# Layer statistics per group instead of per batch of four, and Q and Wo projections interleaved with attention mixing

## The chip, the cores and the metric

One Trainium2 chip, all eight cores; every core runs the same program on its own half of one of four sequences. The metric is the device time in microseconds of the slowest core.

## The reference, cut to what matters

```python
xn = layernorm(x)                                  # (4, 4096, 1024)
def attn(x):
    K = elu(x @ Wk + bk) + 1;  Q = elu(x @ Wq + bq) + 1;  V = x @ Wv + bv    # 16 heads of 64
    KV = einsum('nshd,nshm->nhmd', K, V);  Ksum = K.sum(axis=1)
    Z = 1 / (einsum('nlhd,nhd->nlh', Q, Ksum) + 1e-6)
    out = einsum('nlhd,nhmd,nlh->nlhm', Q, KV, Z) @ Wo + bo
    x = layernorm(x + out) * g1 + beta1
    return layernorm(x + relu(x @ W1 + b1) @ W2 + b2) * g2 + beta2
def experts(x):                                    # 8 experts of width 4096, two per token by a hash of x[:, :2]
    return sum(w[e] * (relu(x @ W1[e] + b1[e]) @ W2[e] + b2[e]) for e in range(8))
out = x + attn(xn) + experts(xn)
```

## The kernel before, in words

A core has 2048 own tokens (`TOWN`, 16 groups of 128, `NGOWN`) and needs K and V of all 4096 tokens of its sequence (32 groups, `NG`). The program is written by hand: the builder emits each engine's instructions in the order of the code, and each engine runs its own list strictly in that order. `em` adds an instruction, `inc` lets it raise a semaphore, `wait` puts a wait in the list, `chain` and `vbar` make an engine wait for its own last instruction. In the code T is TensorE, V VectorE, S ScalarE, G GpSimd (weight loads) and Y the sync engine SP (row loads). `barrier` stands between the stages.

The stages, in order: phase A (statistics, normalization, transposition, K and V, and the sum KV), its tail (routing of the tokens), the experts (`emit_moe`), B1 (`emit_b1`: Q, the attention mixing, Wo), a layernorm, the feed-forward (`emit_b2`), a second layernorm, and the output (`emit_b4`). The change is in phase A and B1 alone.

**Phase A** (`emit_phase_a`) goes by groups, and by batches of four groups for the statistics. Four slots of `xtm_a` hold the rows. For one group g:

- `stats_sums(g)` loads the rows (SP; the slot is free when the transposes of g-4 are done), takes their sum on VectorE (L406) and scales it (L408); ScalarE squares the centred rows (L413) and subtracts the mean (L415); VectorE sums the squares (L418), and for own groups copies the mean (L423).
- `stats_finish` does the rest of the variance for four groups at once: one VectorE scaling (L432), Ln and Exp on ScalarE (L435, L437), four small VectorE operations (L440 to L446), and then on ScalarE for each of the four groups the scaling of the rows (L454) and three one-column copies for own groups (L457 to L461).
- `emit_trans(g)` transposes the eight 128x128 blocks on TensorE (L505) in two waves through one PSUM bank, each copied out by ScalarE (L516).
- `emit_proj(g)` is the K matmuls (L527), a bias row (L531), the V matmuls (L539) and a bias row (L543).
- `elu_all(g)` is the maximum on VectorE (L474), the exp on ScalarE (L482), the min-add (L487) and the copy of V (L493) on VectorE.
- `emit_kv(g)` is sixteen small matmuls (L558, L561), which VectorE adds to the running sums (L573 to L575).

In the loop each group g of a batch is emitted as transposes, projections, `stats_sums` of group g+4, elu, KV, and `stats_finish` of the next batch follows the fourth group. Before the loop stand four `stats_sums` and a `stats_finish`. All group-local buffers of elu and KV have two slots.

**B1** works on two halves s of 1024 own tokens. First the Q projection of both halves, eight output blocks n each (L832, 16 matmuls, with the elu in pieces of 512 columns: L845, L850, L854). Then for each half: the mixing, twice (`sub`, 512 columns each): eight denominator matmuls (L876), an addition and a reciprocal on VectorE (L882, L887), and for each of eight head pairs p a matmul that spreads the reciprocal (L894), a ScalarE copy (L900), the mixing matmul (L904) and a VectorE product (L911); then a reload and transposition of the normalized rows (L933, L941, L948); and the Wo projection, eight blocks (L962, with L972 on VectorE). The copy `xnfm` of the normalized rows lies over `xnbf`, the operand of the Q projection, so it can't be written before the last Q matmul.

Of the kernel before, what the change touches and what calls it, by code (L numbers as in the profile page):

```python
# [6 lines left out]
F32 = mybir.dt.float32  # L7
BF16 = mybir.dt.bfloat16
# [60 lines left out]
class KB:  # L69
    def __init__(self, debug=(), ngl=NG, alim=6, moe_e=NEXP, moe_y=True, gser=False, moe_wb=True, emod=NEXP, hblk=10000):  # L70
# [19 lines left out]
        self.s_lx = [mk("lx0"), mk("lx1"), mk("lx2"), mk("lx3")]  # L90
# [69 lines left out]
    def _decl_sbuf(self):  # L160
# [8 lines left out]
        self.sq2 = sb("sq2", [128, 2 * D], F32, 49664, 65536)  # L169
# [9 lines left out]
        self.xtm_a = sb("xtm_a", [128, 4 * D], F32, TR, 196608)  # L179
        self.ktm = sb("ktm", [128, 2 * D], BF16, TR + 16384, 196608)  # L180
        self.vtm = sb("vtm", [128, 2 * D], BF16, TR + 20480, 196608)
        self.elu_a = sb("elu_a", [128, 2 * D], F32, TR + 24576, 196608)
# [50 lines left out]
        self.scol = sb("scol", [128, 8], F32, SZ + 768)  # L233
# [142 lines left out]
    def emit_phase_a(self):  # L376
        ps = self.ps
        NGL = self.ngl
        assert NGL % 4 == 0
        evT = {}; evKV = {}; evKVmm = {}; evA = {}; evXN = {}  # L380
        evK_s = {}; evK_v = {}; evV_v = {}; evDMA = {}; evSQ = {}
        evKmm = {}; evVmm = {}
        evXNw = [0]

        def lhs(c, g):
            if g < NGOWN:
# [3 lines left out]
        def stats_sums(g):  # L390
            own = g < NGOWN
            bpar = (g // 4) % 2
            j = g % 4
            col = bpar * 4 + j
            sl = g % 4
            xt = self.xtm_a[:, sl * D:(sl + 1) * D]
            if g >= 4:
                self.wait("Y", self.s_mm, evT[g - 4])
            evDMA[g] = self.dma("Y", xt, self.xs[g * 128:(g + 1) * 128, :], self.s_lx[g % 4])
            mc = self.scol[:, col:col + 1]  # L400
            ac = self.tpack[:, col:col + 1]
            sq = self.sq2[:, (g % 2) * D:(g % 2 + 1) * D]
            self.wait("V", self.s_lx[g % 4], evDMA[g])
            if g >= 2:
                self.wait("V", self.s_ve, evSQ.get(g - 2, 0))
            self.em("V", lambda v: v.reduce_sum(mc, xt, axis=AXX))  # L406
            self.vbar()
            self.em("V", lambda v: v.tensor_scalar_mul(mc, mc, -INV_D))  # L408
            v_negm = self.inc("V", self.s_ve, 1)
            self.wait("S", self.s_ve, v_negm)  # L410
            if g >= 2:
                self.wait("S", self.s_ve, evSQ.get(g - 2, 0))
            self.em("S", lambda s: s.activation(sq, xt, AF.Square, bias=mc))  # L413
# [896 lines left out]
```

How the kernel before makes its waits and increments, by code:

```python
    def wait(self, e, sem, val):  # L243
        if val > 0:
            self.L[e].append(lambda x, s=sem.h, v=val: x.wait_ge(s, v))
            self.meta[e].append(("wait", sem.name, val))
# [4 lines left out]
        def fn(x, prev=prev, s=sem.h, n=n):  # L251
            prev(x).then_inc(s, n)
```

## Time and profile before

| | us |
|---|---|
| profiled execution, slowest core | 6002.73 |
| its span, first to last instruction (core 4) | 6001.2 |
| timed runs | 6006.98 and 6708.36 |
| their median | 6357.67 |
| phase A: first to last group's transposes | 69.8 to 714.9 |
| experts, first to last matmul | some 800 to 4550 |
| B1 | 4555 to 4940 |

The page gives TensorE 4866.0 us of matmuls (81% of the span), VectorE 1709.8 (28%), ScalarE 1090.0 (18%) and GpSimd 345.8 (6%). The shares are means over stages with different limits, so the prediction reads phase A, the experts and B1 apart. "Granted clock" is the share of TensorE's full 2.4 GHz that the chip let it have.

### The profile page before, as it was taken

The numbers are of one execution on the slowest core, as the hardware profiler recorded it, in microseconds if no ns is written. First come the engines' busy times: TensorE is split into PE (matmuls) and PEld (weight loads), VectorE is DVE, ScalarE is ACT, GpSimd is POOL, SyncE is SP. The second block draws the span as 40 slices with busy tenths as digits, with TensorE's granted clock in tenths as the row PEclk, the third lists the DMA queues.
The fourth block names the chain that finished last, engine by engine and source line by source line (L and its number), as shares of the span: only waits on it lengthen the run. The fifth ranks groups of instructions, "written<-read, shape, count | busy, mean of one in ns | idle before, by whom it ended". The sixth has DMA issues, their size and how long they took to land.

```text
span 6001.2 us, 55303 instructions; the slowest of 8 cores (5960.0 to 6001.2 us)
## 1 busy us (share of the span) xinstructions
PE 4866.0 (81%) x21246; PEld 2145.8 (36%) x21665; DVE 1709.8 (28%) x3231; ACT 1090.0 (18%) x2013; POOL 345.8 (6%) x661
## 2 busy tenths in 40 slices
PE   3565559999999999999999999999996442677752
PEld 1222224444444444444444444444432110233311
DVE  2333312222222222222222222222223225111153
ACT  2333221111111111111111111111111123111120
POOL 1000000000000000000000000000000000000000
PEclk8777789999999999999989999999998665999965
DMA  2000012222222222222222222222212110111103
GB/s 58 25 25 25 11 26 38 38 36 38 39 36 38 39 36 37 39 36 38 39 32 34 39 36 37 39 36 37 38 30 36 42 39 0 28 26 27 26 7 112
DMA packets 105681, 209.46 MB, mean 35 GB/s; under 512 B 12960, under 2 KB 13232, under 8 KB 105424
## 3 DMA queue, kind: packets, MB, share of 16 engines
q0 software_dynamic: 91056, 163.84, 18.0%
q1 hardware_dynamic: 14368, 42.06, 2.1%
q8 instruction: 177, 2.90, 0.2%
q14 instruction: 80, 0.66, 0.0%
HBM read 361.06 MB, written 8.39 MB: 62 GB/s over the span
## 4 chain that ended last, share of the span: by engine, by line
PE 73%; DVE 11%; ACT 7%; DMA 5%; issue 4%; DVEq 0%; POOL 0%; ACTq 0%; SPq 0%; POOLq 0%
PE ps L735 30%; PE ps L773 30%; PE ps L1099 4%; PE ps L1120 4%; DMA xtm_a<-xs 2%; DMA xt_b<-xs 1%; ACT h_b L1109 1%; DMA xtm_b<-xs 1%; PE ps L779 1%; DVE x_sb L1137 1%; PE ps L505 1%; DVE ln_t L1059 1%; DVE ktm L487 1%; DVE vtm L493 1%; DVE elu_a L474 1%
## 5 line engine op out<-in xcount | busy, mean ns | idle before, releaser
L735 PE MATMUL ps<-xnbf,w1s 128*128 128x512 bf16 x8027 | 1829.1, 383 | 63.9 <-DVE wb L720 32.7
L735 PEld LDWEIGHTS ps<-xnbf,w1s 128*128 128x128 bf16 x8192 | 803.2, 99 | 1057.9 <-issue 150.1
L773 PE MATMUL ps<-h_hi,w2s 128*128 128x512 bf16 x4008 | 929.9, 388 | 27.8 <-DVE acc L797 22.9
L773 PE MATMUL ps<-h_lo,w2s 128*128 128x512 bf16 x4015 | 901.5, 379 | 4.3
L797 DVE TENSOR_TENSOR acc<-acc,ps 128x512 f32<-128x512 f32 x992 | 615.1, 682 | 851.3 <-PE ps L773 535.4
L773 PEld LDWEIGHTS ps<-h_hi,w2s 128*128 128x128 bf16 x4096 | 407.5, 100 | 531.5 <-issue 90.8
L745 ACT ACTIVATE h_lo<-ps,eb_sb 128x512 bf16<-128x512 f32 x512 | 310.2, 688 | 1565.9 <-PE ps L735 1565.9
L745 ACT ACTIVATE h_hi<-ps,eb_sb 128x512 bf16<-128x512 f32 x512 | 310.2, 688 | 1467.3 <-PE ps L735 1467.3
L773 PEld LDWEIGHTS ps<-h_lo,w2s 128*128 128x128 bf16 x4096 | 401.0, 98 | 484.6 <-issue 4.9
L753 DVE TENSOR_TENSOR h_lo<-h_lo,wb 128x512 bf16<-128x512 bf16 x512 | 183.3, 420 | 961.0 <-ACT h_lo L745 961.0
L753 DVE TENSOR_TENSOR h_hi<-h_hi,wb 128x512 bf16<-128x512 bf16 x512 | 183.3, 420 | 900.9 <-ACT h_hi L745 900.9
L1099 PE MATMUL ps<-c_bf,w1s 128*128 128x512 bf16 x1003 | 238.8, 395 | 100.9 <-ACT h_b L1109 76.0
L1120 PE MATMUL ps<-h_b,w2s 128*128 128x512 bf16 x1004 | 234.7, 390 | 92.7 <-DVE x_sb L1137 59.1
L293 POOL DMA_DIRECT2D w2s<-ew_pk x256 | 135.7, 530 | 1751.4 <-PE ps L773 1188.4
L293 POOL DMA_DIRECT2D w1s<-ew_pk x256 | 135.9, 531 | 1705.3 <-PE ps L735 1705.3
L505 PE MATMUL ps<-ident,xtm_a 128*128 128x128 f32 x256 | 64.5, 402 | 168.9 <-ACT xn L461 86.7
L1099 PEld LDWEIGHTS ps<-c_bf,w1s 128*128 128x128 bf16 x1024 | 101.5, 101 | 238.9 <-issue 133.4
L1120 PEld LDWEIGHTS ps<-h_b,w2s 128*128 128x128 bf16 x1024 | 100.2, 100 | 227.2 <-issue 119.6
L1137 DVE TENSOR_TENSOR x_sb<-x_sb,ps 128x512 f32<-128x512 f32 x96 | 59.5, 682 | 421.8 <-PE ps L1120 421.8
L1109 ACT ACTIVATE h_b<-ps,b_sb 128x512 bf16<-128x512 f32 x128 | 77.5, 688 | 491.8 <-PE ps L1099 491.8
L941 PE MATMUL ps<-ident,xt_b 128*128 128x128 f32 x128 | 34.8, 428 | 117.6 <-DVE xt_b L933 117.6
L558 PE MATMUL ps<-vtm,ktm 128*128 128x128 bf16 x256 | 31.0, 239 | 104.3 <-DVE vtm L493 104.3
(169 smaller groups left out, 2250.6 us busy)
## 6 DMA issues: line engine op xcount, KB each, us to landing
w1s<-ew_pk POOLq DMA_DIRECT2D x256, 256.0 KB, 3.8
w2s<-ew_pk POOLq DMA_DIRECT2D x256, 256.0 KB, 3.8
xtm_a<-xs SPq DMA_DIRECT2D x32, 512.0 KB, 3.3
xt_b<-xs SPq DMA_DIRECT2D x32, 256.0 KB, 2.6
w1s<-w_pk POOLq DMA_DIRECT2D x32, 256.0 KB, 3.9
w2s<-w_pk POOLq DMA_DIRECT2D x32, 256.0 KB, 3.9
xtm_b<-xs SPq DMA_DIRECT2D x16, 512.0 KB, 4.0
out<-otm_b SPq DMA_DIRECT2D x16, 512.0 KB, 2.9
```

Source lines behind the costliest of these rows:

```text
L293: self.em(e, lambda x, o=out, i=in_: x.dma_start(out=o, in_=i))
L474: self.em("V", lambda v, hh=hh: v.tensor_scalar(rt[:, hh * 512:(hh + 1) * 512], ps[hh][:], 0.0, None, op0=OP.max))
L505: self.em("T", lambda t, c=c, j=j: t.transpose(ps[4][:, j * 128:(j + 1) * 128], xt[:, c * 128:(c + 1) * 128], self.ident[:]))
L735: self.em("T", lambda t, k=k, tt=tt, slot=slot: t.matmul(ps[tt][:], self.w1t(slot, k), self.xnbf[:, k * TOWN + tt * 512:k * TOWN + (tt + 1 ...
L745: self.em("S", lambda s, tt=tt, i=i, hreg=hreg, e=e, n=n: s.activation(hreg[:, i * TOWN + tt * 512:i * TOWN + (tt + 1) * 512], ps[tt][:], ...
L753: self.em("V", lambda v, tt=tt, i=i, hreg=hreg, e=e: v.tensor_mul(hreg[:, i * TOWN + tt * 512:i * TOWN + (tt + 1) * 512], hreg[:, i * TOWN ...
L773: self.em("T", lambda t, j=j, tt=tt, slot=slot, hreg=hreg, lp=last_plain: t.matmul(ps[4 + tt][:], self.w2t(slot, j), hreg[:, j * TOWN + tt ...
L797: self.em("V", lambda v, dst=dst, tt=tt: v.tensor_add(dst, dst, ps[4 + tt][:]))
L1099: self.em("T", lambda t, k=k, tt=tt, slot=slot: t.matmul(ps[tt][:], self.w1t(slot, k), self.c_bf[:, k * TOWN + tt * 512:k * TOWN + (tt + 1 ...
L1109: self.em("S", lambda s, tt=tt, i=i, n=n: s.activation(self.h_b2[:, i * TOWN + tt * 512:i * TOWN + (tt + 1) * 512], ps[tt][:], AF.Relu, bi ...
L1120: self.em("T", lambda t, j=j, tt=tt, slot=slot: t.matmul(ps[4 + tt][:], self.w2t(slot, j), self.h_b2[:, j * TOWN + tt * 512:j * TOWN + (tt ...
L1137: self.em("V", lambda v, x=xsl, tt=tt: v.tensor_add(x, x, ps[4 + tt][:]))
```

## The change

**Phase A.** The batches go. `emit_stats(g)` computes the whole statistic of one group; `xtm_a` has two slots instead of four, and the squares lie in the slot of `elu_a` instead of a buffer of their own. VectorE keeps the two sums and two scalings. Ln, Exp and the five operations that finish the reciprocal deviation are now all on ScalarE, on one column, each waiting for the one before; the row scaling follows. The mean and the deviation of own groups are written in place, so two of the copies go. The statistic of group g+1 is emitted before KV of group g and its transposes, with the elu of g folded into it: the maximum stands ahead of the second sum on VectorE, the exp ahead of Ln on ScalarE. TensorE's order in phase A is the same as before.

**B1.** The code is cut into functions, and the order is: Q of half 0; Q of half 1 with the first mixing of half 0 behind block 3 and the second behind block 7; row reload of half 0; Wo of half 0 with the first mixing of half 1 behind block 3 and the second behind block 7; row reload of half 1; Wo of half 1. No instruction is added or left out.

```diff
-        self.s_lx = [mk("lx0"), mk("lx1"), mk("lx2"), mk("lx3")]
+        self.s_lx = [mk("lx0"), mk("lx1")]
...
-        self.sq2 = sb("sq2", [128, 2 * D], F32, 49664, 65536)
...
-        self.xtm_a = sb("xtm_a", [128, 4 * D], F32, TR, 196608)
+        self.xtm_a = sb("xtm_a", [128, 2 * D], F32, TR, 196608)
...
+            if g >= 2:
+                self.wait("Y", self.s_mm, evT[g - 2])
+            evDMA[g] = self.dma("Y", xt, self.xs[g * 128:(g + 1) * 128, :], self.s_lx[par])
+            mc = self.mstat[:, g:g + 1] if own else self.scol[:, 0:1]
+            rc = self.rstat[:, g:g + 1] if own else self.scol[:, 1:2]
...
+            self.em("V", lambda v, xt=xt, mc=mc: v.reduce_sum(mc, xt, axis=AXX))
+            self.vbar()
+            self.em("V", lambda v, mc=mc: v.tensor_scalar_mul(mc, mc, -INV_D))
...
+            self.em("S", lambda s, xt=xt, sq=sq, mc=mc: s.activation(sq, xt, AF.Square, bias=mc))
+            self.chain("S", self.s_sc)
+            self.em("S", lambda s, xt=xt, mc=mc: s.add(xt, xt, mc))
+            s_sub = self.inc("S", self.s_sc, 1)
+            if mid_v is not None:
+                mid_v()
+            self.wait("V", self.s_sc, s_sub)
+            self.em("V", lambda v, sq=sq, ac=ac: v.reduce_sum(ac, sq, axis=AXX))
+            self.vbar()
+            self.em("V", lambda v, ac=ac: v.tensor_scalar(ac, ac, INV_D, EPS_LN, op0=OP.mult, op1=OP.add))
+            v_ac = self.inc("V", self.s_ve, 1)
+            if mid_s is not None:
+                mid_s()
+            r0 = self.scol[:, 3:4]
+            self.wait("S", self.s_ve, v_ac)
+            self.em("S", lambda s, ac=ac, r0=r0: s.activation(r0, ac, AF.Ln))
+            self.chain("S", self.s_sc)
+            self.em("S", lambda s, r0=r0: s.activation(r0, r0, AF.Exp, scale=-0.5))
+            self.chain("S", self.s_sc)
+            self.em("S", lambda s, rc=rc, r0=r0: s.mul(rc, r0, r0))
+            self.chain("S", self.s_sc)
+            self.em("S", lambda s, rc=rc, ac=ac: s.mul(rc, rc, ac))
+            self.chain("S", self.s_sc)
+            self.em("S", lambda s, rc=rc: s.mul(rc, rc, self.nwc_sb[:, 0:1]))
+            self.chain("S", self.s_sc)
+            self.em("S", lambda s, rc=rc: s.add(rc, rc, self.nwc_sb[:, 1:2]))
+            self.chain("S", self.s_sc)
+            self.em("S", lambda s, rc=rc, r0=r0: s.mul(rc, rc, r0))
+            self.chain("S", self.s_sc)
+            self.em("S", lambda s, xt=xt, rc=rc: s.mul(xt, xt, rc))
...
+                emit_stats(g, mid_v=lambda pg=pg, ek=ek: elu_vmax(pg, ek),
+                           mid_s=lambda pg=pg, ek=ek, ev=ev: (elu_sexp(pg, ek),
+                                                             elu_vtail(pg, ev)))
+                emit_kv(pg)
...
+            ek, ev = emit_T(g)
+            pend.append((g, ek, ev))
...
+        for n in range(KC):
+            qproj_n(0, n)
+        for n in range(KC):
+            qproj_n(1, n)
+            if n == 3:
+                mix_sub(0, 0)
+            if n == 7:
+                mix_sub(0, 1)
+        xnrec(0)
+        for n in range(KC):
+            wo_n(0, n)
+            if n == 3:
+                mix_sub(1, 0)
+            if n == 7:
+                mix_sub(1, 1)
+        xnrec(1)
+        for n in range(KC):
+            wo_n(1, n)
```

ScalarE in phase A, from the copies of group 3 on, before (`ktm` is K after the exp, `tpack` and `scol` hold statistics, `xn` the first two columns):

```order
L516 CAST xnbf<-ps 128x128 x8
L413 ACTIVATE sq_50<-xtm_a,scol 128x1024
L415 ACTIVATE xtm_a<-xtm_a,scol 128x1024
L482 ACTIVATE ktm<-ps 128x512 x2
L435 ACTIVATE tpack<-tpack 128x4
L437 ACTIVATE tpack<-tpack 128x4
L454 ACTIVATE xtm_a<-xtm_a,scol 128x1024
L457 COPY rstat<-scol 128x1
L459 COPY xn_107<-xtm_a 128x1
L461 COPY xn_107<-xtm_a 128x1
```

and the same engine now, in every step of an own group:

```order
L407 ACTIVATE elu_a<-xtm_a,mstat 128x1024
L409 ACTIVATE xtm_a<-xtm_a,mstat 128x1024
L517 ACTIVATE ktm<-ps 128x512 x2
L422 ACTIVATE scol<-scol 128x1
L424 ACTIVATE scol<-scol 128x1
L426 ACTIVATE rstat<-scol 128x1
L428 ACTIVATE rstat<-rstat,scol 128x1
L430 ACTIVATE rstat<-rstat,nwc_sb 128x1
L432 ACTIVATE rstat<-rstat,nwc_sb 128x1
L434 ACTIVATE rstat<-rstat,scol 128x1
L436 ACTIVATE xtm_a<-xtm_a,rstat 128x1024
L439 COPY xn_106<-xtm_a 128x1
```

Seven one-column activations stand between the exp and the row scaling of each group; before, two on four columns stood there once in four groups.

VectorE in phase A before, one step (`kvacc`, `ksacc` are the running sums):

```order
L406 TENSOR_REDUCE scol<-xtm_a 128x1
L408 TENSOR_SCALAR scol<-scol 128x1
L418 TENSOR_REDUCE tpack<-sq_50 128x1
L423 COPY mstat<-scol 128x1
L474 TENSOR_SCALAR elu_a<-ps 128x512 x2
L487 SCALAR_TENSOR_TENSOR ktm<-ktm,elu_a 128x512 x2
L493 CAST vtm<-ps 128x512 x2
L573 TENSOR_TENSOR kvacc<-kvacc,ps 128x512
```

and now:

```order
L400 TENSOR_REDUCE mstat<-xtm_a 128x1
L402 TENSOR_SCALAR mstat<-mstat 128x1
L505 TENSOR_SCALAR elu_a<-ps 128x512 x2
L414 TENSOR_REDUCE scol<-elu_a 128x1
L416 TENSOR_SCALAR scol<-scol 128x1
L528 SCALAR_TENSOR_TENSOR ktm<-ktm,elu_a 128x512 x2
L534 CAST vtm<-ps 128x512 x2
L563 TENSOR_TENSOR kvacc<-kvacc,ps 128x512
```

The elu maximum (L474, now L505) no longer has both sums ahead of it, but the second sum now stands between it and the min-add.

TensorE in B1 at the end of the first mixing of half 0, before:

```order
L894 MATMUL ps<-zbfb,e_sb 128x512
L904 MATMUL ps<-q_sb,m_sb 128x512
L876 MATMUL ps<-q_sb,ksbd 16x512 x8
L894 MATMUL ps<-zbfb,e_sb 128x512
L904 MATMUL ps<-q_sb,m_sb 128x512
```

and now:

```order
L888 MATMUL ps<-zbfb,e_sb 128x512
L898 MATMUL ps<-q_sb,m_sb 128x512
L834 MATMUL ps<-xnbf,w1s 128x512 x64
L869 MATMUL ps<-q_sb,ksbd 16x512 x8
L888 MATMUL ps<-zbfb,e_sb 128x512
L898 MATMUL ps<-q_sb,m_sb 128x512
```

Sixty-four matmuls, the Q projection of blocks 4 to 7 of half 1, stand between the two mixings that followed each other before.

## Rows read from the trace of the kernel before

**Rows 1.** Stage table: stretch, its us, then busy us (instructions) by engine, clock, DMA.

```profile
240.00:325.00 85.00, 50.97 (x236) 23.31 (x240) 32.15 (x57) 27.01 (x66) 0.00 (x0) 0.74 0.08 25
...
2900.00:3000.00 100.00, 99.53 (x456) 45.34 (x464) 28.82 (x60) 17.78 (x30) 7.42 (x14) 1.00 0.26 40
...
3100.00:3200.00 100.00, 99.27 (x371) 39.59 (x377) 22.04 (x44) 12.12 (x20) 5.83 (x11) 0.81 0.19 30
```

**Rows 2.** Timeline (start us, us, what): TensorE's transposes of groups 0, 29 and 31.

```profile
69.79 1.09 PE L505 MATMUL ps<-ident,xtm_a 128*128 128x128 f32 x4 [69.79 <-ACT xn L461]
...
681.24 0.64 PE L505 MATMUL ps<-ident,xtm_a 128*128 128x128 f32 x4
...
714.91 0.64 PE L505 MATMUL ps<-ident,xtm_a 128*128 128x128 f32 x4
```

**Rows 3.** Waits of phase A, and the row load's time to landing from the page.

```profile
DVE scol L406 <- DMA xtm_a<-xs: 192.6, 28, 14.9
...
xtm_a<-xs SPq DMA_DIRECT2D x32, 512.0 KB, 3.3
```

**Rows 4.** Timeline of the close of the third batch, up to the next transposes.

```profile
326.51 0.16 DVE L432 TENSOR_SCALAR tpack<-tpack 128x4 f32<-128x4 f32 x1
326.77 0.20 ACT L435 ACTIVATE tpack<-tpack 128x4 f32<-128x4 f32 x1 [5.88 <-DVE tpack L432]
...
328.44 1.15 ACT L454 ACTIVATE xtm_a<-xtm_a,scol 128x1024 f32<-128x1024 f32 x1 [1.17 <-DVE scol L446]
329.68 0.19 ACT L457 COPY rstat<-scol 128x1 f32<-128x1 f32 x1
329.96 0.19 ACT L459 COPY xn<-xtm_a 128x1 f32<-128x1 f32 x1
...
330.68 1.09 PE L505 MATMUL ps<-ident,xtm_a 128*128 128x128 f32 x4 [5.62 <-ACT xn L461]
```

**Rows 5.** Timeline of group 28, in the last batch: V matmuls and elu.

```profile
674.71 3.63 PE L539 MATMUL ps<-wv_sb,xnp 128*128 128x512 bf16 x16
674.96 1.29 DVE L474 TENSOR_SCALAR elu_a<-ps 128x512 f32<-128x512 f32 x2 [14.45 <-PE ps L531]
...
677.58 1.29 DVE L487 SCALAR_TENSOR_TENSOR ktm<-ktm,elu_a 128x512 bf16<-128x512 bf16 x2 [1.34 <-ACT ktm L482]
...
679.05 1.29 DVE L493 CAST vtm<-ps 128x512 bf16<-128x512 f32 x2 [0.17 <-DVE ktm L487]
```

**Rows 6.** Timeline of the start: table load and second sum of group 0.

```profile
42.98 1.28 ACT L413 ACT_TABLE_LOAD   x1 [42.98 <-DVE scol L408]
...
46.76 1.22 DVE L418 TENSOR_REDUCE tpack<-sq 128x1 f32<-128x1024 f32 x1 [3.86 <-ACT xtm_a L415]
48.08 0.15 DVE L423 COPY mstat<-scol 128x1 f32<-128x1 f32 x1
```

**Rows 7.** Groups of ScalarE: exp of 512 columns without and with an SBUF bias.

```profile
L482 ACT ACTIVATE ktm<-ps 128x512 bf16<-128x512 f32 x64 | 34.7, 594 | 119.6 <-DVE elu_a L474 119.6
...
L850 ACT ACTIVATE q_sb<-ps,bq_sb 128x512 bf16<-128x512 f32 x32 | 22.0, 687 | 179.0 <-DVE elu_r L845 177.2 <-PE ps L832 1.7
```

**Rows 8.** B1: timeline of the mixings of half 0 and 1; chain of waits (first Wo matmuls, reload).

```profile
4646.90 0.69 DVE L882 TENSOR_SCALAR ps<-ps 16x512 f32<-16x512 f32 x1 [3.83 <-PE ps L876]
...
4662.32 3.58 PE L876 MATMUL ps<-q_sb,ksbd 128*16 128x512 bf16 x8
...
4666.01 0.69 DVE L882 TENSOR_SCALAR ps<-ps 16x512 f32<-16x512 f32 x1 [2.64 <-PE ps L876]
...
4758.10 5.13 PE ps L962 x15
...
4790.67 1.89 PE L876 MATMUL ps<-q_sb,ksbd 128*16 128x512 bf16 x8
...
4828.83 2.71 DMA xt_b<-xs
```

**Rows 9.** Cores view: the die that did not hold the slowest core.

```profile
die 0 (median of its cores): 5973.9 us, clock 0.901
```

More of the change, by code:

```diff
@@ L411, in stats_sums @@
             if g >= 2:
-                self.wait("S", self.s_ve, evSQ.get(g - 2, 0))
-            self.em("S", lambda s: s.activation(sq, xt, AF.Square, bias=mc))
+                self.wait("S", self.s_mm, evKVmm.get(g - 2, 0))
+            self.em("S", lambda s, xt=xt, sq=sq, mc=mc: s.activation(sq, xt, AF.Square, bias=mc))
             self.chain("S", self.s_sc)
-            self.em("S", lambda s: s.add(xt, xt, mc))
+            self.em("S", lambda s, xt=xt, mc=mc: s.add(xt, xt, mc))
             s_sub = self.inc("S", self.s_sc, 1)
+            if mid_v is not None:
+                mid_v()
@@ L511, in emit_trans @@
                 self.wait("S", self.s_mm, mmv)
-                if (g >= NGOWN) and g >= 2:
+                if (not own) and g >= 2:
                     self.wait("S", self.s_mm, evKVmm.get(g - 2, 0))
@@ L546, in emit_proj, with elu_vmax @@
                     start=False, stop=True))
-            evVmm[g] = self.inc("T", self.s_mm, 1)
+            evVmm = self.inc("T", self.s_mm, 1)
+            return evKmm, evVmm
+        def elu_vmax(g, evKmm):
+            par = g % 2
+            rt = self.elu_a[:, par * D:(par + 1) * D]
+            self.wait("V", self.s_mm, evKmm)
+            if g >= 2:
+                self.wait("V", self.s_mm, evKVmm.get(g - 2, 0))
+            for hh in range(2):
+                self.em("V", lambda v, hh=hh, rt=rt: v.tensor_scalar(
+                    rt[:, hh * 512:(hh + 1) * 512], ps[hh][:], 0.0, None, op0=OP.max))
+            evK_v[g] = self.inc("V", self.s_ve, 1)
@@ new lines, in elu_sexp @@
+        def elu_sexp(g, evKmm):
+            par = g % 2
+            kslot = self.ktm[:, par * D:(par + 1) * D]
+            self.wait("S", self.s_mm, evKmm)
+            self.wait("S", self.s_ve, evK_v[g])
+            if g >= 2:
+                self.wait("S", self.s_mm, evKVmm.get(g - 2, 0))
+            for hh in range(2):
+                self.em("S", lambda s, hh=hh, kslot=kslot: s.activation(
+                    kslot[:, hh * 512:(hh + 1) * 512], ps[hh][:], AF.Exp))
+            evK_s[g] = self.inc("S", self.s_sc, 1)
@@ new lines, in elu_vtail @@
+        def elu_vtail(g, evVmm):
+            par = g % 2
+            kslot = self.ktm[:, par * D:(par + 1) * D]
+            vslot = self.vtm[:, par * D:(par + 1) * D]
+            rt = self.elu_a[:, par * D:(par + 1) * D]
+            self.wait("V", self.s_sc, evK_s[g])
+            for hh in range(2):
+                self.em("V", lambda v, hh=hh, kslot=kslot, rt=rt: v.scalar_tensor_tensor(
+                    kslot[:, hh * 512:(hh + 1) * 512], kslot[:, hh * 512:(hh + 1) * 512],
+                    1.0, rt[:, hh * 512:(hh + 1) * 512], op0=OP.min, op1=OP.add))
+            self.vbar()
+            self.wait("V", self.s_mm, evVmm)
+            for hh in range(2):
+                self.em("V", lambda v, hh=hh, vslot=vslot: v.tensor_copy(
+                    vslot[:, hh * 512:(hh + 1) * 512], ps[2 + hh][:]))
+            evV_v[g] = self.inc("V", self.s_ve, 1)
@@ L920, in emit_b1, with xnrec @@
+        def xnrec(s):
+            self.wait("T", self.s_sc, evZB[0])
+            self.wait("Y", self.s_ve, aoz_done[s])
             if s == 1:
```

395 lines of the change are left out of this document (155 added, 240 removed).

## The prediction

> **What bounds the kernel now.** I read the stage table first. In the mixture-of-experts stage TensorE is busy 99.5 of 100 us at a granted clock of 1.00, the upper of its two levels (1.2 and 2.4 GHz) [rows 1]. The change leaves that stage alone, so the edit can only win in phase A and in B1. In a batch of phase A (240 to 325 us) TensorE is busy 51 of 85 us, VectorE 32, ScalarE 27: no engine is full, the stage is a chain. Its length: the first transposes of group 0 start at 69.79, those of group 31 at 714.91 [rows 2]: 645.1 us over 31 steps, 20.8 each. The last batch (groups 28 to 31), beside which no statistics run, steps faster: transposes at 681.24 and, two groups later, at 714.91 [rows 2], 16.84 each. So some 4 us a step belong to how the statistics are placed. The waits show where: VectorE's first sum of a group waited for the row load 28 times, 192.6 us in all [rows 3] (the load waits for the transposes four groups back, so it lands in mid-projection, and the elu maximum is queued behind that whole statistic). And at each batch's end there is the close [rows 4]: from `stats_finish` at 326.51 to the next transposes at 330.68, 4.2 us in which TensorE has nothing, then four row scalings on ScalarE in front of the copies of the first group.
>
> **Phase A, a step of the changed kernel.** The per-step order on TensorE stays (transposes, K, V, KV), so I start from the last batch, which is a step without statistics. Measured from the elu maximum at 674.96: the min-add at +2.62, the copy of V at +4.09, the next transposes at +6.28 (681.24) [rows 5]. Now the statistics of group g+1 go around this. The row load has two slots and starts when the transposes of g-1 are done, most of a step (16.8 us) before its use, and takes 3.3 us to land [rows 3]: nothing waits. First sum, square and subtract run during transposes and K, hidden by TensorE. What lies on the path comes behind the maximum:
> - VectorE: the maxima take 1.29 for two, less an overlap: the second sum starts at +1.25. It takes 1.22 and a step of 1.32 to the next instruction (a sum at 46.76, the next at 48.08) [rows 6], so the one-column scaling starts at +2.57. The min-add, ready at +2.62, slips by under 0.1.
> - ScalarE: hand-off 0.26 (326.51 to 326.77); Ln takes 0.20 there and a copy 0.19, and copies follow each other by 0.28 (329.68, 329.96) [rows 4], so Ln and Exp are 0.29 each. Then five operations of one column with an operand in SBUF. No such row exists. Bounds: 0.28 each, as the copies, and 0.38: the form with an SBUF bias costs 0.093 more on 512 columns (687 against 594 ns) [rows 7]. Mul and add here read such an operand, so I take 0.38: 1.90 us. The row scaling takes 1.15, the signal to TensorE, an estimate, half a hand-off: 0.13. Sum: 2.57+0.26+0.58+1.90+1.15+0.13 = +6.59, against +6.28 for the KV path: 0.31 late. An own group (0 to 15) adds two copies at their spacing, 0.56: 0.87 late.
>
> So the new wait is the transposes on ScalarE's chain, 0.3 to 0.9 us a step; queued behind them is all of TensorE. Steps: 15 of 16.84+0.87 = 17.71 (groups 1 to 15) and 16 of 16.84+0.31 = 17.15: 265.7+274.4 = 540.1 us instead of 645.1, a gain of 105.0. With 0.28 an operation the chain is 0.5 shorter (own 17.21, other 16.84): 527.6, a gain of 117.5.
>
> The start: group 0 no longer waits for four statistics. Its second sum starts at 46.76 and the scaling at 48.08 [rows 6]; then 0.26+0.58+1.90+1.24 (the scaling's spacing, 328.44 to 329.68)+0.28+0.19+0.13 = 4.58 gives transposes at 52.7 instead of 69.79: gain 17.1. The step behind it is in the count above. Phase A's tail is unchanged.
>
> The Trainium skill speaks against this part. "ScalarE: Activation LUTs", section "Table sets: the hidden batching unit", says to batch calls by table set; "What ACT_TABLE_LOAD costs" gives about 2.66 us a switch with its drain. The same page names a set with both ln and exp. The trace has a single load, 1.28 us, at 42.98 [rows 6], though Ln, Exp and Square alternate in every batch, so one set holds all three here and I charge nothing; by the page's price, two switches a group would take back 31 x 5.3 = 165 us, an estimate, and the time would be 6044.
>
> **B1.** Moving the second half's Q projection and the Wo projection around the mixing overlaps little, because the mixing passes every pair through TensorE, ScalarE and VectorE in lockstep and each queue keeps its order: the projection's matmuls stand behind the mixing's last one. What is hidden is the denominator's matmuls, which VectorE waited 3.83 and 2.64 us for [rows 8]; they now run while it finishes elu pieces. Lost: after `mix_sub(0,0)` elu is idle until the first 16 matmuls have run, and those start at the lower clock. After such a stretch 15 took 5.13 [rows 8], with the sixteenth 5.5, less about 0.9 that TensorE is done ahead: 4.6. Gain 3.83+2.64-4.6, some 1.7 with hand-offs. On the Wo side mixing costs 38.1 us in one piece (4790.67 to 4828.8). In two, each begins behind a warm projection, where the eight denominator matmuls take 1.89 and not 3.58 [rows 8]: 17.6 (4790.67 to the next denominator at 4808.31, an estimate from the chain's rows) +18.7 (to its last product, 1.1 later), plus 5.13-3.6 for a Wo restart at the lower clock: 37.8, gain 0.3. B1 together 2; bounds -2 (at the lower clock throughout, by the 3.58 for eight 7.2 for sixteen, twice) and +9 (no restart loss at all). The row reload (`xnrec`, 75 us twice) is the costliest part of B1 and only moves.
>
> **Sum.** 105.0+17.1+2 = 124.1 from the profiled execution's 6002.73: **5879 us**. The faster timed run was 6006.98; the median shown, 6357.67, is the mean of that and 6708.36, and I forecast an execution like the profiled one.
>
> **Clock.** In the profiled execution the slowest core was at 0.81 from 3100 to 3200 us (371 matmuls, against 456 in 100 us at 1.00) [rows 1], and die 0, without that, has a median span of 5973.9 [rows 9], 27 less. If that stretch is absent the forecast is 5852; the range goes below for this and the cheap bound.
>
> **Rivals.**
> - *V falls to the lower clock* (12%). V's 16 matmuls take 3.63 [rows 5], the upper level. If longer idle ahead of the transposes let the clock stay low through K and V, V takes 7.2 (two times 3.58), its copy comes about 3.3 later, and ScalarE's chain hides behind it: 31 x 3.3 less the 18.0 charged above = 84: 5963, within 2%. Against it: idle grows by under 1 us, and K to V is gapless.
> - *The limiter holds a die* (3%), the slower side. 100 us at 0.81 lose 85 of 456 matmuls, 18.6 us [rows 1]. Above 670 us of it my gain is gone, above 1310 us the kernel is slower by 2%; over the 3650 us of experts it is 680 us: 6559. Against it: nearly all windows there show 1.00. The Trainium skill ("TensorE: Matmul & The Clock Gate", section "Seeing it yourself") has a peak-current limiter that takes a die to 13/16 of its clock under dense matmuls on several cores for as long as the load lasts. By that rule, the trace disagrees: only the one stretch shows 0.81.
> - *Table loads in each group* (3%). If the new order makes the compiler pick other sets, two loads of 1.28 a group fall in the chain: 31 x 2.57 = 80, 5959; four, with Square and the elu's exp, 5.1 x 31 = 159: 6038, slower by 0.6%. It decides from 124.1/31 = 4.0 us a group.
> - *The change does little*: ScalarE's chain grows by another 2 us a group, from hand-offs between one-column operations that no row shows (7%): 62 less, 5941.
>
> **Chances.** Forecast case 75%. It lies just beyond the 2% line (120 us, about what a measurement of this kernel can tell from no change), by 4 us, and an error of that size lands on the near side; but the two open points, the cheap bound and the absent 0.81 stretch, both push to the far side, so I give it 0.60 of the 0.75. Faster by over 2%: 0.60; within: 0.36; slower: 0.04. Range 5835 (cheap bound 12.5, the stretch's 27, and some B1) to 5938 (near the last rival).
>
> **What would show it.** Transposes of group 0 at 52.7; a step of 17.2 to 17.7; no 4 us close; the row-load wait gone from VectorE; transposes waiting for ScalarE by 0.3 to 0.9; one table load; five one-column operations at 0.38 spacing; B1 unchanged within 5 us. Wrong if a step exceeds 18.5, or if the clock in V is 0.5.

## The result and the profile after

The changed kernel's executions have a median of 6131.57 us (13 runs, 5850.66 to 6772.67), those of the kernel before, taken beside them, 6716.59 (10 runs, 6006.98 to 6888.22). In many executions of either kernel one die, or two cores of it, run at a lower clock for a time and end up to some 900 us later, the profiled one of the changed kernel among them (die 0, in the view below). What follows is read from core 4 of the changed kernel and compared with cores of before that don't show it; the ratio, taken the same way between executions, is **0.9758, with a 95% interval of 0.9639 to 0.9877**: 2.4% faster. The interval reaches 0.9877, so a gain is shown; that it is more than 2% is likely, and not shown.

Forecast were 5879 us in a range of 5835 to 5938. The median over all executions lies far above that range; the five executions that the ratio is taken from (5850.66, 5878.28, 5883.04, 5884.44, 5922.2; 5884.44 was recorded beside the 13) lie in it.

The cores view of the changed kernel: span, mean granted clock.

```profile
core 0: 6128.2 us, clock 0.854
...
core 4: 5847.0 us, clock 0.907
...
die 1 (median of its cores): 5839.6 us, clock 0.908
```

Die 1 has a median of 5839.6, where before's die 0 had 5973.9 [rows 9]: 134.3 less. Where it came from is read from core 4.

TensorE's transposes, as the view of the tile `xtm_a` sums them up (ns min/median/max, first and last start):

```profile
L455 PE MATMUL ps<-ident,xtm_a x256: 272/421/449, 49.8 to 587.9; 128*128 128x128 f32 x128
```

The last of them starts at 587.9, in before's same view at 717.1. So phase A ends 129.2 us earlier; 20.0 of this is the start (49.77 instead of 69.79 [rows 2]) and 109.2 the 31 steps. From its end the experts take what they took: first matmul to the first Q matmul 3731.7 us, on before's core 0 3729.4. B1, from the first Q matmul (4401.69) to the end of VectorE's last product of Wo (4778.83), went from 380.7 to 377.1.

The start, timeline of ScalarE and VectorE for group 0, to compare with [rows 6] and [rows 4]:

```profile
40.04 1.28 ACT L407 ACT_TABLE_LOAD   x1 [40.04 <-DVE mstat L402]
...
43.82 1.22 DVE L414 TENSOR_REDUCE scol<-elu_a 128x1 f32<-128x1024 f32 x1 [3.86 <-ACT xtm_a L409]
...
45.98 0.29 ACT L426 ACTIVATE rstat<-scol 128x1 f32<-128x1 f32 x1
46.37 0.29 ACT L428 ACTIVATE rstat<-rstat,scol 128x1 f32<-128x1 f32 x1
...
47.92 1.15 ACT L436 ACTIVATE xtm_a<-xtm_a,rstat 128x1024 f32<-128x1024 f32 x1
...
49.77 1.09 PE L455 MATMUL ps<-ident,xtm_a 128*128 128x128 f32 x4 [49.77 <-ACT xn L441]
```

There is one table load in the whole program. A one-column operation takes 0.29 and the next starts 0.39 after it. The close of a batch [rows 4], with its four scalings in a row, is gone.

One step later in the program (group 1 into group 2; the K matmuls of the steps start at 71.61 and 88.78, 17.17 apart; a block of 16 shown as x15 has one record missing, here its first):

```profile
71.61 4.95 PE L475 MATMUL ps<-wk_sb,xnbf 128*128 128x512 bf16 x15 [1.60 <-ACT xnbf L466]
...
77.02 3.63 PE L487 MATMUL ps<-wv_sb,xnbf 128*128 128x512 bf16 x16
...
77.20 1.29 DVE L505 TENSOR_SCALAR elu_a<-ps 128x512 f32<-128x512 f32 x2 [7.99 <-PE ps L479]
78.41 1.21 DVE L414 TENSOR_REDUCE scol<-elu_a 128x1 f32<-128x1024 f32 x1
...
79.97 0.20 ACT L422 ACTIVATE scol<-scol 128x1 f32<-128x1 f32 x1 [0.30 <-DVE scol L416]
...
82.49 1.15 ACT L436 ACTIVATE xtm_a<-xtm_a,rstat 128x1024 f32<-128x1024 f32 x1
...
84.45 0.63 PE L455 MATMUL ps<-ident,xtm_a 128*128 128x128 f32 x4 [0.83 <-ACT xn L441]
```

From the elu maximum at 77.20 the second sum is at +1.21, Ln at +2.77, the row scaling at +5.29 and the next transposes at +7.25. The waits of phase A (50 to 600 us; engine, waited for, us in total, times, longest) show the same over all groups:

```profile
DVE elu_a L505 <- PE ps L479: 258.3, 32, 13.3
...
PE ps L455 <- ACT xn L441: 61.7, 16, 49.8
...
PE ps L548 <- DVE vtm L534: 54.0, 31, 2.1
```

VectorE no longer waits for a row load (192.6 us in [rows 3]). The small KV matmuls wait 54.0 us for the copy of V; in before's core 0 that row reads 99.0. The transposes of own groups wait for ScalarE's last copy: 61.7 less the first one's 49.8 is 11.9 over 15, 0.8 each.

Not every step is like the one shown. From first transposes to first transposes the 31 steps take 16.6 to 18.9 us. Two of them, 18.85 and 18.86, lie above the 18.5 at which the prediction had called itself wrong; in both K's matmuls took 6.1 to 6.2 us instead of the 4.95 above.

### The profile page after: what moved, and what is told of

It reads as the page before. It is cut to its first block, busy times and chain, and to the rows that moved or that the text cites. A ratio compares the mean times of both kernels' runs of the same rounds, so it can differ in the third digit from the quotient of the medians.

```text
span 6130.0 us, 55999 instructions; the slowest of 8 cores (5833.0 to 6130.0 us)
## 1 busy us (share of the span) xinstructions
PE 5169.3 (84%) x21665; PEld 2202.6 (36%) x21665; DVE 1699.1 (28%) x3207; ACT 1139.6 (19%) x2205; POOL 344.4 (6%) x661
## 3 DMA queue, kind: packets, MB, share of 16 engines
q0 software_dynamic: 91056, 163.84, 17.5%
## 4 chain that ended last, share of the span: by engine, by line
PE 81%; DVE 8%; ACT 4%; DMA 3%; issue 3%; POOL 0%; DVEq 0%; SPq 0%; ACTq 0%; POOLq 0%
PE ps L726 31%; PE ps L764 31%; PE ps L1134 4%; PE ps L1113 4%; PE ps L475 3%; PE ps L487 2%; DMA xt_b<-xs 1%; ACT h_b L1123 1%; DMA xtm_b<-xs 1%; PE ps L770 1%; PE ps L455 1%; DVE x_sb L1151 1%; PE ps L957 1%; DVE ln_t L1073 1%; DVE vtm L534 1%
## 5 line engine op out<-in xcount | busy, mean ns | idle before, releaser
L726 PE MATMUL ps<-xnbf,w1s 128*128 128x512 bf16 x8192 | 1961.5, 401 | 53.3 <-DVE wb L711 32.0
L726 PEld LDWEIGHTS ps<-xnbf,w1s 128*128 128x128 bf16 x8192 | 830.9, 102 | 1149.8 <-issue 524.9
L764 PE MATMUL ps<-h_hi,w2s 128*128 128x512 bf16 x4096 | 980.9, 401 | 22.5 <-DVE acc L788 22.5
L764 PE MATMUL ps<-h_lo,w2s 128*128 128x512 bf16 x4096 | 965.2, 397 | 0.0
L764 PEld LDWEIGHTS ps<-h_lo,w2s 128*128 128x128 bf16 x4096 | 414.6, 101 | 529.2 <-issue 196.9
L505 DVE TENSOR_SCALAR elu_a<-ps 128x512 f32<-128x512 f32 x64 | 41.2, 686 | 263.6 <-PE ps L479 263.6
```

The lines of the kernel that those rows point to most:

```text
L726: self.em("T", lambda t, k=k, tt=tt, slot=slot: t.matmul(ps[tt][:], self.w1t(slot, k), self.xnbf[:, k * TOWN + tt * 512:k * TOWN + (tt + 1 ...
L764: self.em("T", lambda t, j=j, tt=tt, slot=slot, hreg=hreg, lp=last_plain: t.matmul(ps[4 + tt][:], self.w2t(slot, j), hreg[:, j * TOWN + tt ...
```

## The experiments

Times of experiments are given as the spans of the cores of the profiled execution, beside before's 5973.9 and the changed kernel's 5839.6, and as a ratio to runs of the kernel before on the same chip where there is one.

### The two parts alone

`a_only` has the changed phase A and the old B1, `b_only` the old phase A and the changed B1.

`a_only`, against the changed kernel (`b_only` has these lines the other way round, against the kernel before):

```diff
-        for n in range(KC):
-            qproj_n(0, n)
-        for n in range(KC):
-            qproj_n(1, n)
-            if n == 3:
-                mix_sub(0, 0)
...
+        for s in range(2):
+            for n in range(KC):
...
+        for s in range(2):
...
+            for sub in range(2):
```

> The changed kernel with B1 as it was before. Theory (phase A brings nearly all of it, because the mixing stays in lockstep): phase A as in the changed kernel (transposes of the first to the last group some 538 us apart), B1 about 3.6 us longer than in the changed kernel; a core that shows no 0.81 stretch ends near 5844, against 5840 for the changed kernel and 5973 before. Rival (interleaving the projections with the mixing hides work): it ends at 5860 or later.

> The kernel before with only B1 rearranged. Theory: from the first Q matmul to the last Wo matmul 3 to 4 us less than before, and an undisturbed core ends near 5969 instead of 5973: no difference that a time can tell. Rival: the interleaving is worth 15 us or more, 5958 or less. Second rival: the restarts at the lower clock cost more than the hidden denominators give, above 5973.

`a_only`: spans of 5843.4 to 5854.3, ratio 0.9782 (0.9737 to 0.9828), transposes from 49.3 to 588.6. `b_only`: spans of 5956.9 to 5972.2 on die 0 (to 5992.3 on die 1, at a clock of 0.895 to 0.897), ratio 0.9983 (0.9961 to 1.0006), transposes from 70.0 to 719.4. Phase A is the change. By its time B1 alone can't be told from nothing, but the trace has its size: from the first Q matmul to the end of B1 the eight cores take 374.2 to 377.4 us, in before 378.6 to 383.1. The two add up: 0.9782 x 0.9983 = 0.9765, against 0.9758.

### What in phase A gave the gain

Two kernels take one idea each into the kernel before. `max_first` puts the elu maximum ahead of the second sum on VectorE and leaves the batches:

```diff
             s_sub = self.inc("S", self.s_sc, 1)
+            if mid is not None:
+                mid()
             self.wait("V", self.s_sc, s_sub)
             self.em("V", lambda v: v.reduce_sum(ac, sq, axis=AXX))
...
-                    stats_sums(nxt[j])
+                    stats_sums(nxt[j], mid=lambda g=g: elu_max(g))
```

> The kernel before, batches kept, with one thing moved on VectorE: the elu maximum stands ahead of the second sum of the statistic instead of behind it. Theory (a part of the 4 us a step is the maximum queued behind a statistic whose rows land late): a step inside a batch falls from about 18.5 to about 17.1, 28 steps by 1.4 are 39 us, an undisturbed core ends near 5934. Rival (all of it was the close of the batch): no change, 5973.

`spread` leaves VectorE alone and scales each group's rows a step ahead of its transposes instead of all four in the close:

```diff
                 emit_trans(g)
                 emit_proj(g)
+                if j < 3:
+                    scale_rows(g + 1)
```

> The kernel before, batches kept, with one thing moved on ScalarE: at the close only the first group's rows are scaled; the other three are scaled one by one behind the copies of the group before. Theory (the close costs both the finish of the statistics and three scalings in front of the copies): the interval across a close falls by 4.9 us for own groups and 2.6 for the others, about 30 in all, an undisturbed core ends near 5943. Rival (the scalings only move and come back as a later wait in the step): 5973.

`max_first` has spans of 5914.9 to 5921.0 (one execution), 55 less than before, where some 39 had been expected. `spread` has 5932.7 to 5950.5, 33 less, as expected, and a ratio of 0.9945 (0.9909 to 0.9982). The waits of phase A (same columns as above). Before, core 0:

```profile
DVE scol L406 <- DMA xtm_a<-xs: 192.5, 28, 15.1
DVE tpack L418 <- ACT xtm_a L415: 76.6, 29, 2.6
PE ps L558 <- DVE vtm L493: 99.0, 31, 4.7
```

`max_first`:

```profile
DVE scol L406 <- DMA xtm_a<-xs: 197.1, 28, 15.5
DVE tpack L420 <- ACT xtm_a L415: 3.1, 2, 2.6
PE ps L563 <- DVE vtm L498: 56.5, 31, 2.5
```

`spread`:

```profile
DVE scol L406 <- DMA xtm_a<-xs: 164.6, 28, 9.5
PE ps L561 <- DVE vtm L496: 102.7, 31, 4.4
```

The big wait, VectorE's for the row load, is still whole in `max_first`, and yet 55 us are gone: it was no bound in itself. What bound the step was the elu, and with it the copy of V and the KV matmuls, queued behind the second sum, which itself waited for ScalarE (76.6 us over 29 times in before, 3.1 now). Moving the maximum takes 42.5 us off the KV matmuls' wait, nearly down to the 54.0 of the changed kernel. The expectation had priced the sum alone (1.4 us a step) and not that wait in front of it. In `spread` the KV matmuls' wait stays, and the time comes from the copies behind the transposes (TensorE's wait for the copy `xnbf` ahead of the second wave is 36.0 us in before and 16.2 here). The start of 20.0 and these two make 108 of the 129 us. What is left, some 21, belongs to the rest of the close; that the parts add is argued, not tested.

The same can be read from TensorE's timelines. The table has the mean over the steps of groups 1 to 30, us. V's matmuls take 3.63 in every step of all these cores.

| | step | first transposes to V | end of V to next transposes |
|---|---|---|---|
| before, core 0 | 20.7 | 11.4 | 5.7 |
| `max_first`, core 0 | 19.0 | 11.1 | 4.2 |
| `spread`, core 0 | 19.8 | 10.3 | 5.8 |
| changed kernel, core 4 | 17.3 | 10.0 | 3.6 |
| `more_ops`, core 0 | 20.3 | 11.1 | 5.6 |
| `no_newton`, core 0 | 16.2 | 9.7 | 2.9 |
| `keep_busy`, core 0 | 15.7 | 8.2 | 3.8 |

`max_first` gains behind V, `spread` ahead of it, and the changed kernel has both and some 0.6 us more behind V, in 31 steps some 20, about what was left. The granted clock of 60 to 560 us differs too (0.75 before, 0.78, 0.76, and 0.79 changed), so a part of these gains can be the clock's; no run separates it.

### The new chain on ScalarE

To see how much of the step the one-column operations hold, `no_newton` drops all five (they refine the reciprocal deviation; the output then rests on Exp of Ln alone), and `more_ops` puts five more of their kind behind them, whose result nothing reads.

`no_newton`:

```diff
-            self.em("S", lambda s, r0=r0: s.activation(r0, r0, AF.Exp, scale=-0.5))
-            self.chain("S", self.s_sc)
-            self.em("S", lambda s, rc=rc, r0=r0: s.mul(rc, r0, r0))
...
-            self.em("S", lambda s, rc=rc, r0=r0: s.mul(rc, rc, r0))
+            self.em("S", lambda s, rc=rc, r0=r0: s.activation(rc, r0, AF.Exp, scale=-0.5))
```

`more_ops`, these two lines five times:

```diff
             self.em("S", lambda s, rc=rc, r0=r0: s.mul(rc, rc, r0))
             self.chain("S", self.s_sc)
+            self.em("S", lambda s, r0=r0, ac=ac: s.mul(self.dum[:, 6:7], r0, ac))
+            self.chain("S", self.s_sc)
```

> The changed kernel without the five one-column operations behind Exp (the step that refines the reciprocal deviation is left out). Theory (the transposes wait for ScalarE's chain by 0.8 us in a step of an own group and 0.3 in the others, 16.6 us in all, and the KV path stands right behind): the chain is 1.9 shorter, the KV path is late everywhere, 16 to 17 us less, an undisturbed core near 5823. Rival 1 (the chain is hidden): 5840. Rival 2 (the chain bounds every step fully): 31 x 1.9 = 59 less, 5781.

> The changed kernel with five more one-column operations with an SBUF operand in the chain (their result isn't used). Theory (TensorE waits for this chain in every step): each costs 0.386 a step, 31 steps by 1.93 are 60 us and the start 2 more, an undisturbed core near 5902. Rival (there is slack): less than 20 us.

`no_newton`: spans of 5802.5 to 5810.2, ratio 0.9749 (0.9686 to 0.9812): 34 less than the changed kernel where 17 were expected. `more_ops`: 5932.8 to 5947.8, 100 more than the changed kernel where 62 were expected. Both miss on the same side: the direction is that of the chain, the size is more than the chain. In the table above, `more_ops` loses 2.0 us a step behind V, where the chain is, and 1.1 ahead of V, where nothing was edited; `no_newton` gains 0.7 and 0.4. In `more_ops` the direct part is as worked out. Timeline of one step of it (the view ends within the last block):

```profile
322.32 5.76 PE L485 MATMUL ps<-wk_sb,xnbf 128*128 128x512 bf16 x15 [1.60 <-ACT xnbf L476]
...
328.55 3.63 PE L497 MATMUL ps<-wv_sb,xnbf 128*128 128x512 bf16 x16
328.80 1.29 DVE L515 TENSOR_SCALAR elu_a<-ps 128x512 f32<-128x512 f32 x2 [10.74 <-PE ps L489]
...
337.99 1.09 PE L465 MATMUL ps<-ident,xtm_a 128*128 128x128 f32 x4 [2.76 <-ACT xn L451]
...
342.77 5.56 PE L485 MATMUL ps<-wk_sb,xnbf 128*128 128x512 bf16 x14 [1.60 <-ACT xnbf L476]
```

Maximum to next transposes is 9.19, against 7.25 in the step shown above: +1.94, which is five operations at 0.39. But the step is 20.45 against 17.17. The other 1.3 are on TensorE, in work that nobody touched: transposes to K 4.78 against 4.33, K to V 6.23 against 5.41. TensorE's own groups over phase A (busy us, mean ns of one | idle), and the granted clock of that stretch (us, PE busy, PEld, DVE, ACT, POOL, clock), say it for all groups. `more_ops`:

```profile
L465 PE MATMUL ps<-ident,xtm_a 128*128 128x128 f32 x196 | 53.1, 426 | 88.2 <-ACT xn L451 41.8 <-ACT xtm_a L446 21.7 <-ACT xnbf L476 15.1
...
60.00:560.00 500.00, 328.84 (x1463) 146.61 (x1485) 193.53 (x325) 234.98 (x645) 0.00 (x0) 0.75 0.08 26
```

The changed kernel, core 4:

```profile
L475 PE MATMUL ps<-wk_sb,xnp 128*128 128x512 bf16 x207 | 70.7, 516 | 23.4 <-ACT xnp L466 23.4
...
L455 PE MATMUL ps<-ident,xtm_a 128*128 128x128 f32 x232 | 52.9, 371 | 46.3 <-ACT xnbf L466 15.1 <-ACT xnp L466 14.9 <-ACT xn L441 11.9
...
60.00:560.00 500.00, 355.84 (x1706) 160.42 (x1734) 224.61 (x377) 233.43 (x610) 0.00 (x0) 0.79 0.09 31
```

`no_newton`:

```profile
L445 PE MATMUL ps<-ident,xtm_a 128*128 128x128 f32 x240 | 44.2, 314 | 31.1 <-ACT xnp L456 16.0 <-ACT xnbf L456 15.1
...
60.00:540.00 480.00, 347.98 (x1747) 153.99 (x1776) 230.22 (x388) 197.04 (x479) 0.00 (x0) 0.84 0.10 32
```

A transpose takes 426, 371 and 314 ns as the chain gets shorter, and the stretch's granted clock is 0.75, 0.79 and 0.84, between the levels of 1.2 and 2.4 GHz. In `no_newton` no wait of the transposes for the statistics is left; the KV path is what bounds it. And its steps are of two kinds. K of two groups that follow each other:

```profile
309.57 5.75 PE L465 MATMUL ps<-wk_sb,xnp 128*128 128x512 bf16 x15 [1.75 <-ACT xnp L456]
...
326.17 3.40 PE L465 MATMUL ps<-wk_sb,xnp 128*128 128x512 bf16 x15 [1.52 <-ACT xnp L456]
```

In seven of the 31 steps K's fifteen take 3.40, and these steps last 14.1 to 14.3 us; all others but the first two last 16.8 to 17.2. Of these two the first has a granted clock of 0.80 (305.39 to 322.32 us) and the second of 1.00 (322.32 to 336.56). The same instructions, in the same order, differ by some 2.6 us a step with the level of the clock.

### Is it the clock?

This could still be something else that grows with the step. `keep_busy` leaves the changed kernel's chain whole and fills TensorE's idle time ahead of and between the transposes with spare matmuls of 384 columns, whose results land in PSUM banks not in use at that moment and are read by nobody: six behind V, two and four behind the two transposition waves. So that they overwrite nothing that is still read, the transposes also wait for the elu maximum and exp of the group before (those lines are not shown).

```diff
+        def busy(n, bank):
+            for i in range(n):
+                self.em("T", lambda t: t.matmul(
+                    ps[bank][:, 0:384], self.wk_sb[:, 0:128], self.wk_sb[:, 0:384],
+                    start=True, stop=True))
...
                 evXNw = self.inc("S", self.s_sc, 1)
+                busy(2 if wave == 0 else 4, 0)
...
             evVmm = self.inc("T", self.s_mm, 1)
+            busy(6, 4)
```

> The changed kernel with spare matmuls of 384 columns in TensorE's idle time of a step of phase A (six behind V, two behind the first and four behind the second wave of transposes; their results are never read). Theory (the step answers to ScalarE's chain by more than the chain's own length because TensorE's idle time before K sets at which level its clock runs in the transposes and in K): the transposes and K run at the upper level, K's 16 matmuls take about 3.6 instead of 5.4 us, the step falls by 1.5 to 2.3 us, 47 to 70 us in all, an undisturbed core near 5780. Rival 1 (the clock doesn't answer to idle of this size, or K is slow for another reason): the spare matmuls hide or delay a little, 5840 to 5860. Rival 2 (the spare matmuls end late and push the transposes): slower than 5860.

Spans of 5784.7 to 5798.6, 49 less than the changed kernel (47 to 70 had been expected), at a ratio of 0.9745 (0.9721 to 0.9768); transposes end at 539.6 instead of 587.9. And that with 88.6 us more of matmuls in phase A. The group of the spare matmuls, one step's K, and the clock over phase A:

```profile
L447 PE MATMUL ps<-wk_sb 128*128 128x384 bf16 x370 | 88.6, 369 | 0.0
...
326.23 3.61 PE L485 MATMUL ps<-wk_sb,xnp 128*128 128x512 bf16 x16 [0.66 <-ACT xnp L475]
...
60.00:540.00 480.00, 406.51 (x2208) 187.76 (x2207) 237.84 (x400) 246.07 (x644) 0.00 (x0) 0.93 0.10 33
```

K's sixteen matmuls take 3.61 us in half of the steps and 4.0 to 5.4 in the others, where fifteen took 4.95 above, and the clock is 0.93. So the changed kernel paid for the clock with at least some 1.6 us in each of 31 steps (538.1 less 490.0), on top of the waits that its chain shows. By the table it is 1.8 ahead of V, less 0.2 that the spare matmuls and the added waits cost behind it. `more_ops` and `no_newton` moved along that same price.

### A reload with two slots, and the best of all

In B1 the row reload was named the costliest part. It loads 32 pieces, each into the one buffer `xt_b1`, when the transposes of the piece before are done. `two_slots` gives it a second buffer.

```diff
-                    xt = self.xt_b1[:]
-                    if xf_prev[0] or xf_prev[1]:
-                        self.wait("Y", self.s_mm, max(xf_prev))
+                    xt = self.xt_b1[sl][:]
+                    if xf_prev[sl]:
+                        self.wait("Y", self.s_mm, xf_prev[sl])
```

> The changed kernel with two slots instead of one for the reloaded rows in B1. Theory (B1 is bound by the reload: 32 pieces in series of load 2.6 to 3, normalization 0.55, transposes 1.1, 4.7 us each with hand-offs; the interleaving left that untouched): two pieces in flight, 75 us fall to about 38 per half, 74 us less in all, an undisturbed core near 5766. Rival (the loads queue behind each other or the copies on ScalarE bound it): less than 30 us.

Spans of 5765.7 to 5781.6, 67 less than the changed kernel (74 had been expected), ratio 0.9703 (0.9615 to 0.9792). Timeline of VectorE's scalings of the reload, in the changed kernel:

```profile
4526.19 0.55 DVE L928 TENSOR_SCALAR xt_b<-xt_b,mstat,rstat 128x512 f32<-128x512 f32 x1 [3.15 <-DMA xt_b<-xs]
...
4531.03 0.55 DVE L928 TENSOR_SCALAR xt_b<-xt_b,mstat,rstat 128x512 f32<-128x512 f32 x1 [4.29 <-DMA xt_b<-xs]
```

In `two_slots`:

```profile
4528.88 0.55 DVE L929 TENSOR_SCALAR xt_b<-xt_b,mstat,rstat 128x512 f32<-128x512 f32 x1 [4.18 <-DMA xt_b<-xs]
4529.34 0.54 DVE L929 TENSOR_SCALAR xt_b1b<-xt_b1b,mstat,rstat 128x512 f32<-128x512 f32 x1
...
4533.81 0.55 DVE L929 TENSOR_SCALAR xt_b<-xt_b,mstat,rstat 128x512 f32<-128x512 f32 x1 [3.94 <-DMA xt_b<-xs]
```

Two pieces now pass in 4.9 us, where one took 4.8. VectorE still waits some 4 us of these for the load.

`best` adds to this a refinement of four operations instead of five (Square, and one Identity with scale and bias), and the two copies of own groups behind the release of the transposes instead of ahead of it; a row load then also waits for ScalarE's copies of two groups back. `best_busy` is `best` with the spare matmuls of `keep_busy`.

```diff
-            self.em("S", lambda s, rc=rc: s.mul(rc, rc, self.nwc_sb[:, 0:1]))
-            self.chain("S", self.s_sc)
-            self.em("S", lambda s, rc=rc: s.add(rc, rc, self.nwc_sb[:, 1:2]))
+            self.em("S", lambda s, rc=rc: s.activation(rc, rc, AF.Identity, scale=-0.5, bias=self.nwc_sb[:, 1:2]))
...
             self.em("S", lambda s, xt=xt, rc=rc: s.mul(xt, xt, rc))
+            evA[g] = self.inc("S", self.s_sc, 1)
             if own:
```

> The changed kernel with the two reload slots, the refinement in four operations instead of five, and the two one-column copies of own groups behind the release of the transposes. Theory: two_slots' 74 us and the 16.6 us of the waits for ScalarE, which the chain being 0.5 us shorter and the copies 0.56 us out of the way take away: an undisturbed core near 5750. Rival: the copies come back as a wait of the PSUM copies behind them and only 5 us of the 16.6 are gained.

> The version with two reload slots, the shorter chain and the copies out of the way (an undisturbed core at 5735), with the same spare matmuls. Theory: as keep_busy, less what the shorter idle already gave: the step falls from 16.3 by 1 to 2 us, 31 to 62 in all, an undisturbed core near 5690. Rival: 5735 or more.

`best`: 5732.2 to 5742.1 on cores 0 to 3, 6 and 7 (5848.1 on core 4), 38 less than `two_slots` where 17 had been expected, again with a higher clock of phase A (0.84), ratio 0.9609 (0.9561 to 0.9657). `best_busy`: spans of 5671.8 to 5689.1, median 5699.64 of four runs (5683.66 to 5711.35), ratio **0.9535 (0.9506 to 0.9564)**; near 5690 had been expected. It beats both kernels. One step of it:

```profile
328.70 3.61 PE L486 MATMUL ps<-wk_sb,xnp 128*128 128x512 bf16 x16 [0.63 <-ACT xnp L476]
...
333.03 1.29 DVE L517 TENSOR_SCALAR elu_a<-ps 128x512 f32<-128x512 f32 x2 [4.92 <-PE ps L490]
```

## Why the prediction was right or wrong

**The time.** For an execution like the profiled one the forecast was 5879 with the 0.81 stretch of before's core 4 and 5852 without it. The stretch is absent on the changed kernel's core 4 (3100 to 3200 us at a clock of 1.00), and the span is 5847.0. The ratio is 0.9758 (forecast 5879/6002.73 = 0.9794), on the side of 2% that the likeliest case had, but with an interval that reaches across that line. **What failed is the step from this to the time of the kernel**: "I forecast an execution like the profiled one". One of the two executions shown was 6708.36, and a range that leaves such executions out can't hold a median over all of them; 6131.57 lies 194 above its end. The rival of a held die was priced well (6559; executions of 6525 to 6773 were seen), but it was given 3% and tied to the change, while the kernel before has the same executions. The argument against it, that nearly all windows show 1.00, came from one execution and said nothing of the others: nine of the 14 recorded ones of the changed kernel have a die that ends 130 us or more later. What holds the clock down in them, no run here tells.

That 5847.0 lies so near 5852 is in part luck. The start, the steps and B1 together gave 8.7 us more than forecast, and against before's core 0 this core lost 2.3 in the experts and 5.7 behind B1, where nothing was changed.

**The start**: 17.1 forecast, 20.0 measured. The chain from the second sum to the transposes was right: 52.7 forecast less 46.76 is 5.9, and 49.77 less 43.82 is 6.0. What was missed is that the second sum itself comes 3 us earlier (43.82 instead of 46.76 [rows 6]).

**The steps**: 105.0 forecast, 109.2 measured. Row scaling +5.29 (forecast 2.57+0.26+0.58+1.90 = 5.31), next transposes of an own group +7.25 (forecast 6.59+0.56 = 7.15); waits of 0.8 and, for the others, 4.7 us over 14, 0.3 (forecast 0.87 and 0.31); 0.39 for a one-column operation (0.38 taken, the upper bound). The mean step of an own group is 17.5 where 17.71 was forecast (17.17 is the commonest, and a few are longer where K is slow), that of the others 17.0 where it was 17.15: the base of 16.84, taken from the last batch, was too long by 0.1 us.

**The base taken as fixed.** The same step of the working shows the reasoning's real gap. It took TensorE's part of a step as given and added ScalarE's lateness. The runs show TensorE's part moving with the idle time ahead of it: an edit of the chain by 1.9 us a step gave 3.3. At the change's own size (waits of some 0.5) the error is small and fell on the good side; at the 2.8 us of `more_ops` it is not (100 us instead of 62).

**B1**: gain of 2 forecast (bounds -2 and +9), 3.6 measured. The two waits of VectorE for the denominators, 3.83 and 2.64 [rows 8], are gone, and the elu of half 1 waits once for its first Q matmuls:

```profile
4487.08 0.75 DVE L847 TENSOR_SCALAR elu_r<-ps,bq_sb 128x512 bf16<-128x512 f32 x1 [4.05 <-PE ps L834]
...
4614.90 1.90 PE L869 MATMUL ps<-q_sb,ksbd 128*16 128x512 bf16 x8
```

4.05 against a forecast 4.6. On the Wo side the denominators run at the upper clock, 1.90 us for eight, as forecast. `b_only` confirms the size by its trace, 376.8 us on core 0 against before's 380.7, and not by its time.

**The rivals.** V did not fall to the lower clock: its sixteen matmuls take 3.63 on core 4, as before. The rival looked at the wrong block. What the idle time costs is in the transposes and in K, and the argument against it ("idle grows by under 1 us") is what kept it small. Table loads in each group: one load in the program, 1.28 us. The Trainium skill's batching by table set ("ScalarE: Activation LUTs", "Table sets: the hidden batching unit") took nothing here: by the single load, one set holds all the functions used. ScalarE's chain longer by 2 us a group: it is what `more_ops` built, and it costs 100 us, not the 62 of that rival.

## What to carry to other kernels

A long wait in the table of waits is not a bound by itself: VectorE waited 193 us for a load, and moving two instructions one place up in the queue behind it, ahead of a sum that waits for another engine, gave 55 us with the wait untouched. Ask what is queued behind each waiting instruction and who waits for that. And where TensorE idles for a us or two in each short step, price an edit of the chain by the measured step with more and with less of it, since the clock adds to the chain's own time; spare matmuls in those gaps can be worth more than a shorter chain.

## What the runs showed of the hardware

- The clock's part in a step that is a chain was not expected. With gaps of 0.8 to 2 us K's sixteen matmuls took about 5.3 us (an estimate; fifteen in 4.95) and the stretch had 0.79; with most of them filled 3.61 in half of the steps, and 0.93. With 2.8 us ahead of the transposes fifteen took 5.76, at 0.75. Filling the gaps of the changed kernel was worth 49 us of a phase of 540. The Trainium skill ("TensorE: Matmul & The Clock Gate", section "What's actually happening") says that the default state is throttled and activity releases the throttle; by that, filling the gaps should help, and the trace agrees.
- Filling these gaps took TensorE's time from nobody on the cores read here: V stayed at 3.63, and VectorE's wait for TensorE ahead of the elu maximum shrank from 258.3 to 209.1 (50 to 600 us of the changed kernel, core 4, and of `keep_busy`, core 0).
- Cores 4 and 5 of `keep_busy` and 0 and 1 of `best_busy` had V at 4.38 in their first ten steps, and core 0 of `best_busy` a granted clock of 0.81 from 60 to 200 us. Cores 4 and 5 of `best`, which has no spare matmuls, show ten such steps too. In `keep_busy` this cost next to nothing (first to last transposes 491.3 and 491.9, on the other cores 486.9 to 493.1), in `best_busy` some 17 (465.7 and 465.3, the others 447.9 to 450.8).
- Five more one-column operations on ScalarE cost their spacing of 0.39 us each in the chain: each takes 0.29 and 0.10 pass before the next, which waits for it.
